# Householder tridiagonalisation on one core: x times the stored pairs summed on VectorE, and the corrections of e moved into the scalar chain

## The reference, cut to what matters

```python
deg = jnp.sum(A, axis=0) + jnp.sum(A, axis=1) - jnp.diagonal(A)
d_inv_sqrt = jnp.where(deg > 0, jax.lax.rsqrt(deg), 0.0)
L_norm = d_inv_sqrt[:, None] * (jnp.diag(deg) - A) * d_inv_sqrt[None, :]
_, U = jnp.linalg.eigh(L_norm)
agg = jnp.einsum('mn,bnd->bmd', U.T, features)
```

## Time and profile before

| | us |
|---|---|
| median of 3 runs (6368.24 to 6369.15) | 6369.11 |
| the profiled execution: its own time | 6370.36 |
| its span in the trace | 6368.6 |
| PE busy / DVE busy / ACT busy | 4002.2 / 4479.3 / 1270.0 |
| the 510 Householder steps (from the first to past the last) | 2844.60 |
| of these DVE busy / PE busy | 2196.80 / 1822.88 |

### The profile page before, as it was taken

The page is one execution under the profiler, slowest core; times in us unless marked ns, Lnnn a source line. Parts: engine busy times, 40 slices in busy tenths (PEclk is TensorE's granted clock), DMA queues, the critical chain, the costliest instruction groups (busy, mean ns, idle before and its releaser), DMA issues. The chain is left out here.

```text
span 6368.6 us, 81910 instructions
## 1 busy us (share of the span) xinstructions
PE 4002.2 (63%) x23728; PEld 2741.1 (43%) x23728; DVE 4479.3 (70%) x24648; ACT 1270.0 (20%) x3608; POOL 16.8 (0%) x30
## 2 busy tenths in 40 slices
PE   5777766666666655553333333358788699995684
PEld 5667665555555555551000000023342465553352
DVE  6777777777787877778999999941223777724457
ACT  1111211111122222222222222212432111110100
POOL 0000000000000000000000000000000000000000
PEclk9855555555555555555555555569899599997876
DMA  1000000000000000000000000000000000000000
GB/s 34 2 2 2 2 1 1 1 1 1 1 1 1 1 1 1 1 1 0 0 0 0 0 0 0 0 21 0 0 0 0 0 0 0 0 0 0 0 1 27
DMA packets 14096, 17.20 MB, mean 3 GB/s; under 512 B 624, under 2 KB 10000, under 8 KB 13712
## 3 DMA queue, kind: packets, MB, share of 16 engines
q1 hardware_dynamic: 10896, 9.44, 0.5%
q10 hardware_dynamic: 2352, 2.69, 0.2%
q0 software_dynamic: 464, 0.55, 0.0%
HBM read 8.47 MB, written 4.19 MB: 2 GB/s over the span
## 5 line engine op out<-in xcount | busy, mean ns | idle before, releaser
L497 PE MATMUL coef<-vwv 128*128 128x40 f32 (+28 forms) x2476 | 665.7, 396 | 199.2 <-DVE x_parts L422 199.2
L497 PEld LDWEIGHTS coef<-vwv 128*128 128x128 f32 x2476 | 600.2, 326 | 213.3 <-issue 213.3
L792 DVE SCALAR_TENSOR_TENSOR poly<-poly,off,term 128x60 f32<-128x60 f32 x2560 | 609.5, 274 | 0.0
L784 DVE SCALAR_TENSOR_TENSOR term<-cut,rows,poly 128x60 f32<-128x60 f32 x2560 | 597.6, 275 | 9.8
L715 PE MATMUL both_signs<-signs,identb 128*128 128x480 bf16 x320 | 186.2, 582 | 564.8 <-PEq L65 564.8
L554 PE MATMUL totals<-pp_sum,ones 128*128 128x2 f32 x768 | 225.3, 363 | 469.1 <-DVE pp_sum L408 469.1
L1003 PE MATMUL horner_ps<-horner,S 128*128 128x512 f32 x1024 | 460.6, 592 | 0.0
L554 PEld LDWEIGHTS totals<-pp_sum,ones 128*128 128x128 f32 x768 | 192.3, 311 | 508.0 <-DVE pp_sum L408 508.0
L515 PEld LDWEIGHTS product<-x_parts,A_parts 128*128 128x128 bf16 x11136 | 379.0, 109 | 43.0 <-DVE A_parts L338 42.7
L515 PE MATMUL product<-x_parts,A_parts 128*128 128x3 bf16 x11136 | 359.3, 167 | 41.7 <-DVE A_parts L338 41.7
L1523 PE MATMUL gate_ps<-h_sb,wih_t 128*128 x504 | 314.1, 783 | 81.9 <-PEq L65 81.9
(11 more groups left out here) (481 smaller groups left out, 7810.5 us busy)
## 6 DMA issues: line engine op xcount, KB each, us to landing
out_dram<-x_sb SPq DMA_DIRECT2D x4, 1024.0 KB, 7.3
adj_sb<-adj_dram SPq DMA_DIRECT2D x1, 1024.0 KB, 5.6
alpha<-L_gnn_alpha_train_dram POOLq DMA_DIRECT2D x1, 256.0 KB, 5.8
edge_row<-L_gnn_src_dram POOLq DMA_DIRECT2D x1, 128.0 KB, 5.7
edge_row<-L_gnn_dst_dram POOLq DMA_DIRECT2D x1, 128.0 KB, 6.2
w<-L_gnn_Wg_dram ACTq DMA_DIRECT2D x2, 64.0 KB, 4.7
w<-L_gnn_W_dram ACTq DMA_DIRECT2D x2, 64.0 KB, 4.1
x_sb<-x_dram SPq DMA_DIRECT2D x4, 0.5 KB, 10.4
```

Of the source, the lines that this page charges most:

```text
L497: last = pe.matmul(coef[:, 0:2 * j].rearrange("p (j t) -> p j t", t=2), vwv[:, c, j % 2, 1:2].broadcast_to([P, P]), vwv[:, c, 2:2 + j, 1:3 ...
L784: pair(dve.scalar_tensor_tensor(out=term[:, way, :], in0=flat, scalar=rows[:, way, row:row + 1], in1=poly[:, b, way, s + 1, :], op0=ALU.su ...
L792: pair(dve.scalar_tensor_tensor(out=poly[:, b, way, s + 2, :], in0=poly[:, b, way, s, :], scalar=off2[:, way, row:row + 1], in1=term[:, wa ...
```

## The change: what it does

1. **coef by one product.** At the end of a step VectorE multiplies the new x into all stored pairs, block by block (`on_pairs`, n x 2(j+1) elements), and sums that over the blocks (a second instruction, which reads the tile across its blocks, 256 bytes apart). TensorE then makes `coef` by one product of ones with these 2(j+1) sums, in place of n products (n >= 2). For n = 1 nothing is to be summed, and coef stays as it was. The last step of a panel needs no sums.
2. **row of e first.** TensorE makes `row_e` as soon as w is there: for n >= 3 ahead of the norm, for n <= 2 right behind it. coef now comes behind the norm (n >= 3, ahead of A times x) or behind A times x (n <= 2).
3. **The order of VectorE's middle.** `prod_e` and `ae` move from behind x_scaled into the scalar chain: prod_e between sgn and q2, ae between q2 and nb. `prod` moves ahead of inv_mask.

The diff, cut to its core:

```diff
@@ -214,6 +214,8 @@
+        on_pairs = sb("x_on_pairs", [P, C, 2 * NB])
+        on_pairs_sum = sb("x_on_pairs_sum", [P, 2 * NB])
...
@@ -359,10 +361,16 @@
                 mark(dve.reciprocal(q, root[:]), "q")
                 dve.wait_ge(column_ready, row + 1)
                 mark(dve.tensor_scalar(sgn, alpha, 0.0, 0.5, ALU.is_ge, ALU.subtract), "sgn")
+                if j:
+                    dve.wait_ge(row_ready, row - row // NB)
+                    mark(scaled(prod_e[:, c0:C, 1:1 + 2 * j], row_e[:, 0:2 * j]), "prod_e")
                 after("q")
                 mark(dve.scalar_tensor_tensor(out=q2, in0=q, scalar=s, in1=root[:], op0=ALU.mult, op1=ALU.add), "q2")
-                if j == 0:
+                if j:
+                    after("prod_e")
+                else:
                     dve.wait_ge(panel_kept, row // NB)
+                mark(dve.tensor_reduce(ae, prod_e[:, c0:C, 0:1 + 2 * j], AX.X, ALU.add), "ae", row)
                 after("q2")
                 mark(dve.tensor_tensor(nb, q2, sgn, ALU.mult), "nb")
                 after("nb")
...
@@ -372,11 +380,12 @@
                 mark(dve.reciprocal(inv_nb, nb), "inv_nb")
                 after("h")
                 mark(dve.reciprocal(tau, h), "tau", row)
+                if j:
+                    dve.wait_ge(coef_ready, row - row // NB)
+                    mark(scaled(prod[:, c0:C, 0:2 * j], coef[:, 0:2 * j]), "prod")
                 after("inv_nb")
                 mark(dve.tensor_scalar(inv_mask[:, c0:C], mask, inv_nb, None, ALU.mult), "inv_mask")
                 if j:
-                    dve.wait_ge(coef_ready, row - row // NB)
-                    mark(scaled(prod[:, c0:C, 0:2 * j], coef[:, 0:2 * j]), "prod")
                     after("prod")
                     mark(dve.tensor_reduce(corr, prod[:, c0:C, 0:2 * j], AX.X, ALU.add), "corr")
                 else:
...
@@ -384,15 +393,8 @@
                 after("inv_mask")
                 mark(dve.scalar_tensor_tensor(out=x_scaled[:, c0:C], in0=x, scalar=tau, in1=inv_mask[:, c0:C], op0=ALU.mult,
                                               op1=ALU.mult), "x_scaled")
-                if j:
-                    dve.wait_ge(row_ready, row - row // NB)
-                    mark(scaled(prod_e[:, c0:C, 1:1 + 2 * j], row_e[:, 0:2 * j]), "prod_e")
-                    after("prod_e")
-                mark(dve.tensor_reduce(ae, prod_e[:, c0:C, 0:1 + 2 * j], AX.X, ALU.add), "ae", row)
-                if j == 0:
-                    after("corr")
+                after("corr")
                 mark(dve.tensor_tensor(to_y[:, c0:C], corr, inv_mask[:, c0:C], ALU.mult), "to_y")
-                after("ae", row)
                 mark(dve.scalar_tensor_tensor(out=side[:, c0:C], in0=ae, scalar=nb, in1=corr, op0=ALU.mult, op1=ALU.add), "to_side")
                 after("to_y")
                 mark(dve.scalar_tensor_tensor(out=to_y[:, c0:C], in0=e_next, scalar=-DELTA, in1=to_y[:, c0:C],
...
@@ -445,6 +447,13 @@
+                if n > 1 and not last:
+                    mark(dve.tensor_tensor(on_pairs[:, c0:C, 0:2 * j + 2].rearrange("p c (j t) -> p c j t", t=2),
+                                           vwv[:, c0:C, 2:3 + j, 1:3],
+                                           x_next.unsqueeze(2).unsqueeze(3).broadcast_to([P, n, j + 1, 2]), ALU.mult), "on_pairs")
+                    after("on_pairs")
+                    mark(dve.tensor_reduce(on_pairs_sum[:, 0:2 * j + 2], on_pairs[:, c0:C, 0:2 * j + 2].rearrange("p c f -> p f c"),
+                                           AX.X, ALU.add), "on_pairs", row + 1)
...
@@ -493,11 +502,13 @@
                                      start=(c == c0), stop=(c == C - 1))
                 last.then_inc(norm_ready, 1)
 
-            def coefs(row, j, c0, c):
-                last = pe.matmul(coef[:, 0:2 * j].rearrange("p (j t) -> p j t", t=2), vwv[:, c, j % 2, 1:2].broadcast_to([P, P]),
-                                 vwv[:, c, 2:2 + j, 1:3], start=(c == c0), stop=(c == C - 1))
-                if c == C - 1:
-                    last.then_inc(coef_ready, 1)
+            def coefs(j, c0):
+                if c0 == C - 1:
+                    pe.matmul(coef[:, 0:2 * j].rearrange("p (j t) -> p j t", t=2), vwv[:, c0, j % 2, 1:2].broadcast_to([P, P]),
+                              vwv[:, c0, 2:2 + j, 1:3], start=True, stop=True).then_inc(coef_ready, 1)
+                else:
+                    pe.matmul(coef[:, 0:2 * j], k.ones[:], on_pairs_sum[:, 0:2 * j], start=True, stop=True)\
+                        .then_inc(coef_ready, 1)
 
             def row_of(row, j, c0):
                 c = (row + 1) // P
...
@@ -530,25 +541,25 @@
                         if j:
                             pe.wait_ge(dve_did, pos["x", row])
                         norm(j, c0)
-                        if j == 0:
-                            pe.wait_ge(dve_did, pos["split", p] if n > 1 else pos["changed", p, C - 1])
-                        elif n > 1:
-                            pe.wait_ge(dve_did, pos["x2", row])
-                        products(c0)
                     if j:
                         pe.wait_ge(dve_did, pos["w", row - 1])
-                    if j and n >= 3:
-                        coefs(row, j, c0, c0)
-                        pe.wait_ge(dve_did, pos["xx", row])
-                    if n >= 3:
-                        norm(j, c0)
-                    if j:
-                        for c in range(c0 + (n >= 3), C):
-                            coefs(row, j, c0, c)
                         row_of(row, j, c0)
                     if n >= 3:
-                        pe.wait_ge(dve_did, pos["x2", row] if j else pos["split", p])
-                        products(c0)
+                        if j:
+                            pe.wait_ge(dve_did, pos["xx", row])
+                        norm(j, c0)
+                        if j:
+                            pe.wait_ge(dve_did, pos["on_pairs", row])
+                            coefs(j, c0)
+                    if j == 0:
+                        pe.wait_ge(dve_did, pos["split", p] if n > 1 else pos["changed", p, C - 1])
+                    elif n > 1:
+                        pe.wait_ge(dve_did, pos["x2", row])
+                    products(c0)
+                    if j and n <= 2:
+                        if n == 2:
+                            pe.wait_ge(dve_did, pos["on_pairs", row])
+                        coefs(j, c0)
                     if n > 1:
                         pe.wait_ge(dve_did, pos["pp", row])
                         pe.matmul(totals[:, 0:2], k.ones[:], pp_sum[:], start=True, stop=True).then_inc(dot_ready, 1)
```

4 lines of the change are left out of this document (2 added, 2 removed).

## The result

| | before | after |
|---|---|---|
| median of 4 runs each, us | 6368.67 (6365.17 to 6369.15) | 6108.40 (6105.19 to 6111.74) |
| ratio, 95% interval | | 0.9593 (0.9576 to 0.9609) |
| the profiled execution: time / span, us | 6370.36 / 6368.6 | 6111.74 / 6110.0 |

The change takes 4.1% off, 260 us.

A forecast was written before the change was run, and what follows sets the result against it. The prediction took VectorE's middle and the end part, not TensorE, to bound each step. Gains of 233 us less 1 for the pair sums gave 232, so 6137 us from 6368.67, with a range of 6118 to 6185.

The forecast's parts named there:

- the end part: From v_y to the next reciprocal: dot product, next x, norm and root; 3.15 us long, forecast to stay unchanged.
- Part 1: On TensorE, row_e takes the first coef product's place ahead of the norm; end part unchanged: 0.
- Part 2: VectorE's middle: same 19 instructions, reordered to cover waits; v_y 2.34 instead of 2.83 us behind the reciprocal.
- Gain 0.48 per step: VectorE's middle at j = 16: shortening from filled pauses, same at larger steps, 0.40 at j = 1 and 2.
- the 233: Gain in us over the steps, from 58 (n = 3), 51 (n = 2), 54 (n = 1), 66 (n = 4), 2 (j = 0).
- All six pauses: VectorE's waits before q2, nb, inv_mask, corr, ae and side at j = 16, sum 0.50 us, all to be filled.
- the rule: VectorE starts: an unheld instruction about 0.08 us before the previous one's end, a waiting one about 0.035 past its end.
- The wait for row_e: At n = 2, row_e follows four half norm products, so prod_e starts at 0.2 to 0.25 us, not 0.15.
- the 8.4: Early n = 4 steps, where TensorE was late: 4.9 us of v_y idle time plus 44 x 0.08.
- The cover: Later tau delays ScalarE's scalings and w; some 2.5 us of room, at most 1 used; otherwise up to 0.47 a step.
- Part 3: Two VectorE instructions for x on the pairs, before the reciprocal: hold it in a few late steps, 1 us in all.
- fillers cover only the hand-over: Rival for VectorE's middle: each of six pauses gives back only 0.04 us, so 6240 us; chance 0.05.

The follow-up runs named there:

- the pair sums alone: The changed kernel with VectorE's middle back in the old order, keeping row_e first, the pair sums and one coef product: 6361.82 us, ratio 0.9988 to before.
- six products of 0.153: The changed kernel plus twelve unused, unheld VectorE instructions per step, six of them plain products, ahead of v's correction: 6724.99 us in one run.

## Why the prediction was off, by its own steps

- **What bounds: right.** VectorE's middle and the end part are the path. With A times x 0.98 us earlier and the old middle, the step did not move (5.98, 5.99).
- **Part 1, the end part unchanged: right.** The norm stands 0.42 behind row_e, as it stood 0.41 behind coef.
- **Part 2, the step that failed: the size of the gain, "Gain 0.48 per step" and the 233 worked from it.** All six pauses were covered, as said, but the steps gained 268 us. At row 16 it was 0.58 a step, not 0.48. In the mean of the steps with j > 0 it was 0.64, 0.56, 0.49 and 0.46 for n = 4, 3, 2 and 1, where the terms were 66/124 = 0.53, 0.47, 0.41 and 0.44. In us: n = 4 79.7 for 66, n = 3 70.4 for 58, n = 2 61.9 for 51, n = 1 56.1 for 54, each with its share of j = 0.
- **Where the 0.09 of row 16 lies.** Forecast and measured starts behind the reciprocal were: prod_e 0.15 and 0.13, q2 0.35 and 0.33, ae 0.48 and 0.46, nb 0.70 and 0.66, tau 1.24 and 1.19, prod 1.32 and 1.25, inv_mask 1.52 and 1.44, corr 1.65 and 1.57, to_y 1.99 and 1.89, v_y 2.34 and 2.25. No single instruction carries the 0.09; it comes in pieces of 0.01 to 0.02. Behind sgn and tau (0.14 long) the next starts after 0.06, as the rule says, where the working had 0.07 and 0.08: a slip that the rows could have shown. Behind ae nb starts after 0.20, not 0.22. And durations changed with the order: the mean of prod went from 230 to 219 ns, of ae and corr from 236 to 230 and 229 (groups by line over the steps); with prod moved back they were 230 for it and 236 for corr again. That no row of before showed.
- **By move:** prod's was put at 0.04 + 0.12 - 0.02 = 0.14 and measured 0.21 at row 16 (5.99 to 5.77), that of prod_e and ae at 0.05 + 0.13 + 0.12 + 0.04 = 0.34 and measured 0.39 (5.99 to 5.60).
- **The wait for row_e: half right.** At n = 2 it was charged with 0.05 to 0.10 and cost 0.045 on average. At n = 1 row_e was to be "done in time"; it is not, and the wait costs the same 0.045. That n = 1 came within 2 us of its term is therefore luck in part: an estimate from 0.045 x 121 steps is that the missed wait took back some 5 us of what the slots gave more.
- **j = 0:** 0.12 was forecast, 0.19 measured. **Early steps of n = 4:** right; j = 1 went from 5.85 to 5.02, and the 8.4 put down for them agrees with the 8.3 of the pair sums alone, although product ended only 3.5 of the 4.9 us of idle time that the prediction gave to it nearly whole.
- **The cover: right.** w, tau and ScalarE never came up: row_e's product starts after the same 0.80 us of idle time as coef's had the earlier trace rows, so w is no later than it was.
- **Part 3: right, and the sum on the safe side.** The working's 0.54 and 0.31 are slots: they fit 0.15 us + 1.87 ns an element, less the 0.08 of overlap, which makes durations of 0.61 and 0.38. Measured were 570 ns at 248 elements and 285 at 124, so slots of 0.49 and 0.21. The reciprocal was never held by them, where 1 us was forecast: it starts 0.03 us behind the root's end at every j from 1 to 31. At row 31 (n = 4), for example, the sum ends at 219.61 and the reciprocal starts at 219.53, just the overlap that a slot allows, with the root done at 219.50. The cacheline note of the Trainium skill, SBUF — State Buffer, in the section on the DMA port swizzle, agrees in direction for four blocks; for two blocks, which are as far apart, there is next to no penalty (285 ns, against 281 for the same sum without gaps).
- **Stages behind the steps "unchanged": wrong** by 8 us, and 1.4 came ahead of the steps. The two hid a quarter of the miss: 233 - 1 - 0 was forecast against 268.1 - 9.5. That the time came as near to the range as 10 us is owed to this, and is luck.
- **The rivals:** that fillers cover only the hand-over falls with the 0.58 a step and with the slots of 0.073 us. By the sentence of the Trainium skill in VectorE: DVE Perf Modes, on the DRAIN, that the next instruction waits for the empty pipe, six products of 0.153 would have taken 0.92 us; they took 0.44. The range was set by what would make the change worse; downward it held 19 us, less than ten roundings of 0.01 in 494 steps (49 us).

## What to carry to other kernels

On a chain of short dependent instructions, what counts is the time from start to start. Moving an independent instruction into a pause wins the part of the pause that it fills, less the pause that opens at its old place: prod behind nb filled 0.12 and opened 0.06 at n = 4, and over all steps it won 0.03 a step. When such a chain is forecast from rows, take each slot from the row of that very instruction, and let the range reach to both sides by the rounding times the number of slots times the number of steps. Moving work off an engine that isn't the bound is worth little alone, and much together with the change that makes it the bound: the pair sums gave 8 us with the old middle and 84 with the new.
